# A decoder stack in two interleaved streams: another order of their steps, and fewer matmuls of constants

## What is computed

```
x = layernorm(x + L0_attn(x))                    causal softmax attention, one head
x = layernorm(x + L0_xattn(x, ctx, ctx, mask))   masked attention on ctx, with its own layernorm
x = layernorm(x + L0_ffn(x))                     256 -> 1024 -> 1024 -> 256, weights of +1 and -1
x = layernorm(x + L1_attn(x))                    linear attention, 16 heads, random features (64)
x = layernorm(x + L1_xattn(x, ctx, ctx))         gated scores of 8 heads with running maximum
x = layernorm(x + L1_ffn(x))                     quantized 256 -> 1024, 3-tap convolution, silu, 1024 -> 256
```

## Time and profile before

| | |
|---|---|
| median of 3 runs | 850.7 us (850.16 to 853.18) |
| profiled execution, span of the core | 848.1 us |
| TensorE busy | 787.7 us, 93% |
| TensorE weight loads (beside the matmuls) | 529.7 us |
| VectorE busy | 573.0 us, 68% |
| ScalarE busy | 355.4 us, 42% |
| GpSimd busy | 150.0 us, 18% |
| mean granted TensorE clock | 0.980 of full |

### The profile page before, as it was taken

The page is one execution under the profiler, slowest core; times in us unless marked ns, Lnnn a source line. Parts: engine busy times, 40 slices in busy tenths (PEclk is TensorE's granted clock), DMA queues, the critical chain, the costliest instruction groups (busy, mean ns, idle before and its releaser), DMA issues.

```text
span 848.1 us, 15194 instructions
## 1 busy us (share of the span) xinstructions
PE 787.7 (93%) x6103; PEld 529.7 (62%) x6171; DVE 573.0 (68%) x1470; ACT 355.4 (42%) x641; POOL 150.0 (18%) x231
## 2 busy tenths in 40 slices
PE   9999999999999889999989999999999979988485
PEld 6766556755676756578754666677556756657233
DVE  2458634762476779968889945466356675788786
ACT  3854213342263237573338433244352233483162
POOL 5011102100015210031420020100026120014200
PEclk9999999999999999999999999999999999999698
DMA  9700000010010000111000030000000000000000
GB/s 354 277 2 1 1 1 0 2 26 2 1 51 26 27 2 2 34 67 51 26 1 1 2 98 1 3 1 2 1 1 1 2 2 2 1 1 2 0 25 26
DMA packets 12742, 23.80 MB, mean 28 GB/s; under 512 B 768, under 2 KB 7040, under 8 KB 12416
## 3 DMA queue, kind: packets, MB, share of 16 engines
q1 hardware_dynamic: 12672, 22.82, 7.8%
HBM read 20.72 MB, written 2.10 MB: 27 GB/s over the span
## 4 chain that ended last, share of the span: by engine, by line
PE 75%; DVE 15%; issue 4%; ACT 3%; POOL 2%; DMA 1%; SPq 0%; DVEq 0%; ACTq 0%; POOLq 0%
PE bank L758 13%; PE bank L568 6%; PE bank L576 5%; PE bank L602 5%; PE bank L623 4%; PE bank L856 4%; PE bank L1097 3%; PE bank L1059 3%; PE bank L554 3%; PE bank L768 3%; PE bank L744 2%; PE bank L837 2%; PE bank L803 2%; PE bank L706 2%; PE bank L561 2%
## 5 line engine op out<-in xcount | busy, mean ns | idle before, releaser
L2084 POOL TENSOR_TENSOR rstd<-rstd,minus_half 128x2 f32<-128x2 f32 x56 | 42.7, 763 | 472.5 <-DVE rstd L1195 472.4
L758 PE MATMUL bank<-work,f0w 128*128 128x512 f16 x512 | 115.5, 379 | 0.1
L758 PEld LDWEIGHTS bank<-work,f0w 128*128 128x128 f16 x512 | 49.3, 98 | 58.8 <-issue 1.6
L1405 DVE SCALAR_TENSOR_TENSOR work<-bank,work 128x512 f16<-128x512 f32 x64 | 42.7, 685 | 48.4 <-ACT work L1907 48.3
L1907 ACT ACTIVATE work<-bank 128x512 f16<-128x512 f32 x64 | 37.0, 597 | 67.1 <-PE bank L758 51.0
L554 PE MATMUL bank<-bar_upper,identb 128*128 128x512 bf16 x201 | 57.7, 398 | 6.9 <-ACT work L1932 2.7
L623 PE MATMUL bank<-work 128*128 128x256 f32 x208 | 50.0, 381 | 0.4 <-DVE work L1302 0.4
L1945 ACT ACTIVATE work<-bank 128x512 f32<-128x512 f32 x32 | 19.1, 596 | 60.9 <-PE bank L856 60.9
L1270 DVE TENSOR_REDUCE small<-bank 128x1 f32<-128x512 f32 (+3 forms) x32 | 18.7, 586 | 35.2 <-PE bank L604 32.2
L623 PEld LDWEIGHTS bank<-work 128*128 128x128 f32 x208 | 38.0, 190 | 7.0 <-issue 1.7
L554 PEld LDWEIGHTS bank<-bar_upper,identb 128*128 128x128 bf16 x235 | 22.3, 103 | 32.0 <-issue 9.2
(11 more groups left out here) (303 smaller groups left out, 1776.1 us busy)
## 6 DMA issues: line engine op xcount, KB each, us to landing
work<-in_mask SPq DMA_DIRECT2D x4, 1024.0 KB, 10.3
xT<-in_xT SPq DMA_DIRECT2D x4, 512.0 KB, 4.8
ctxT<-in_ctxT SPq DMA_DIRECT2D x4, 512.0 KB, 4.8
perf_w<-in_k SPq DMA_DIRECT2D x3, 512.0 KB, 10.1
perf_w<-in_perf_w SPq DMA_DIRECT2D x1, 1536.0 KB, 6.4
x<-in_x SPq DMA_DIRECT2D x2, 512.0 KB, 14.1
ctx<-in_w SPq DMA_DIRECT2D x2, 512.0 KB, 12.2
work<-in_w SPq DMA_DIRECT2D x1, 1024.0 KB, 11.9
```

The costliest lines, as they stand in the source:

```text
L758: ins = nc.tensor.matmul(u.bank[:, :], f0w1[:, k, m * P:(m + 1) * P], s.h1[part][:, k, :], start=(k == 0 and part == 0), stop=(k == NF - 1 ...
L1405: low_part(what, m, dst, number + m, lambda o, x, hi: nc.vector.scalar_tensor_tensor(out=o, in0=x, scalar=0.0, in1=hi, op0=ALU.max, op1=AL ...
L2084: nc.gpsimd.tensor_tensor(s.rstd[:, two], s.rstd[:, two], minus_half[:, 0:2], ALU.pow).then_inc(s.rstd_made.sem, 1)
```

## The change

TURNS is another merged order, on all five queues, and KEEP is another table, whose numbers sum to 36 instead of 235. No other line is changed, so all later lines of the changed kernel stand 14 lines higher (L554 becomes L540). A line or two of each table:

```diff
 TURNS = {
     "tensor":
-        "a8 b1 a4 b1 a6 b2 a2 b1 a13 b3 a1 b4 p1 a2 b1 a3 b2 a4 b1 a2 b1 a1 b1 a6 b1 a2 b1 a4 b1 a4 b2 a3 b1 a2 b2 a2 "
+        "a2 b1 a9 b1 a7 b2 a1 b1 a13 b1 a1 b3 p1 b1 a1 b1 a2 b2 a1 b1 a2 b1 a1 b1 a14 b1 a9 b2 a2 b1 a1 b1 a1 b1 a1 b1 "
...
 KEEP = {
-    "quant.hidden6 0 0": 2, "quant.hidden7 0 0": 3, "quant.topT 0 0": 9, "quant.row2 0 0": 8,
...
+    "self.q 0 0": 2, "cross.q1 0 0": 2, "sign.early 0 0": 1, "perf.ft.1 0 0": 1, "quant.turn0 0 1": 2,
+    "quant.topT 0 1": 2, "perf.ft.0 1 0": 1, "perf.score3.0 1 0": 1, "perf.spread.0 1 0": 1, "perf.fk.1 1 0": 1,
+    "perf.ft.1 1 0": 4, "perf.state.1 1 0": 1, "perf.out1 1 0": 1, "mlstm.xT1 1 0": 2, "quant.hidden5 1 0": 1,
+    "perf.spread.0 1 1": 1, "perf.state.1 1 1": 3, "mlstm.out0 1 1": 1, "quant.turn0 1 1": 1, "quant.turn1 1 1": 1,
+    "quant.hidden0 1 1": 1, "quant.taps0 1 0": 1, "quant.topT 1 1": 4
```

More of the change, by code:

```diff
@@ L37 @@
     "tensor":
[8 rows of a table removed]
[L46 removed]
[11 rows of a table removed]
[L58 removed]
[8 rows of a table removed]
[8 rows of a table added]
+    "vector":
[11 rows of a table added]
+    "scalar":
[8 rows of a table added]
     "gpsimd":
[L68 to L69 removed]
+        "a7 b2 a3 b2 a2 b3 a4 b2 a1 b1 a2 b1 a1 b1 a3 b1 a2 b3 a2 b1 a2 b4 a1 b2 a1 b1 a1 b1 a3 b1 a2 b1 a2 b3 a1 b4 a3 "
+        "w1 b2 a2 b1 a1 b2 a6 b13 a2 b2",
     "sync":
[L71 removed]
+        "w1 a1 w3 b1 a1 w2 a1 b1 a1 w1 b1 w1 b1 a5 b2 a2 b5 a2 b2",
 }
 KEEP = {
[19 rows of a table removed]
[5 rows of a table added]
 }
```

3 lines of the change are left out of this document (removed), and 70 rows, old and new, of tables (KEEP, TURNS).

## The result

The changed kernel takes 846.76 us (median of 20 runs, 841.59 to 851.19), the kernel before 851.62 (20 runs, 848.79 to 854.53). The ratio is 0.9949, interval 0.9933 to 0.9964, which is a gain of 4.3 us (3.1 to 5.7). The profiled execution has a span of 844.5 us beside 848.1 before.

A forecast was written before the change was run, and what follows sets the result against it. TensorE, busy 93% of the span, was taken to bound most of the kernel, VectorE 301 to 361 and 427 to 443 us. Eight stretch terms summed to -9.6 us, giving 841.1 us (837 to 845, chance 0.46; wider range 832 to 854).

The forecast's parts named there:

- the price of 0.215 us: Cost of one constant matmul on TensorE at full clock; all 235 cost some 50 us.
- Stretch 1: 0 to 244 us, TensorE full: 12 constants fewer, forecast -2.4 us.
- Rival A: Freed time turns into TensorE waits, also in stretches called full; 846.9 us, chance 0.24.
- stretches 1, 4 and 6: 0 to 244, 361 to 427 and 443 to 679 us, paced by TensorE: forecast -2.4, -1.3 and -2.8 us.
- Stretch 3: 301 to 361 us, VectorE paces: 66 constants fewer, nearly all hidden, L1502 delays VectorE, clock falls; forecast +1.5 us.
- Stretch 7: 679 to 742 us, mixed waits: 10 constants fewer, about half of their 2.1 us in waits; forecast -1.5 us.
- Stretch 8: 742 us to the end: 60 constants fewer, mostly in waits, gains at row2, heads and an eviction; forecast -2.5 us.
- Stretch 5: 427 to 443 us, VectorE paces: 24 constants fewer give 0, longer low clock costs; forecast +0.4 us.
- Stretch 6: 443 to 679 us, TensorE full: 15 constants fewer give 3.2 us, 0.4 taken back for new waits; forecast -2.8 us.
- the 5 us that I had named as a sign: Any stretch changing by more than 5 us would show the method wrong, the order mattering more than the constants.
- Rival B: Slower through TensorE's low clock, at 301 to 361 us (+13 us) and perhaps the end; 852.4 to 858 us, chance 0.18.
- the two conditions that I gave together: Signs of the clock rival: granted clock below 0.8 in both 301 to 361 us and the last 106 us.

The follow-up runs named there:

- constants_at_second_fall: The changed kernel plus 8 constant matmuls ahead of the first stream's quant.topT in the second round (10 in place of 2): 843.8 us, ratio 0.9912.
- kernels with two and with three places: Changed kernel plus 18 constants, at perf.fq.1/fk.1/ft.1 and first stream's topT, second round: 841.2 us; or plus 36, also at the tail: 840.2 us.

## Why the prediction was right or wrong

- **Which stretches TensorE fills, and the price of 0.215 us there:** right. Stretch 1 gave 3.0 us for 12 constants (2.4 forecast), and 18 constants put into full flow cost 3 to 4 us (3.9 by the price). Rival A, in which half of the freed time of full stretches turns into waits, is out, although its 846.9 us is nearly the measured time: it had 3.3 us for stretches 1, 4 and 6, and they gave 9.8.
- **Stretch 3, hidden behind VectorE, with the delay of L1502 and a short fall of the clock:** right for the sum of 301 to 361 us (+1.1, +1.5 forecast), the row of L1488 shows the wait of 1.39 us, and the clock is 0.89. The low level was on from 302 to 309 and from 332 to 339 us, not in the 8 us after 344, 13.7 us in sum, where I had priced one fall of 4 us. That the sum fits is in part luck.
- **"Stretch 7: 10 fewer, 2.1 us, about half in waits, -1.5":** wrong in sign, +1.0. The step that failed is that I asked of a constant only whether it stood on the path, and took one in a wait for free to remove. The row that I had against the clock (7.3 us of idle time in this stretch and still 1.00) was one with the constants in place; without them the waits of 0.7 us became 1.9 and 1.5, and the clock went to 0.53 for 11 us. Putting them back made the stretch 2.5 us shorter in one profile, and together with those of stretch 8 the whole 5 us shorter by the runs (0.9885 beside 0.9949).
- **"Stretch 8: -1.3, -1.1, -0.4, +0.3 for a lower clock near the end":** three gains by order and constants were outweighed by a term that I had at 0.3 us. Measured +2.5, 5.0 us off. The step that failed is the same one: I took the nine constants at row2 as 1.3 us on the path, and the clock of the steps behind them as given. The 1.3 us came (cols start 1.5 us earlier behind the gates), and cols at the lower level took 2.4 us again. Of the 1.1 us at the heads 0.9 appears where the clock is full. I had also read the nine as running at the low clock; the low level ended while they ran, at 755.70 us. For the rest of the stretch I can't say term by term what the clock took: the low intervals lie differently in every execution.
- **"Stretch 5: +0.4":** mis-sized, +2.5. Giving back the old order took 1.5 us off this stretch (+1.0 in place of +2.5), 20 constants in its wait took nothing. The other 1.0 us is there in the old order with the new constants too (+1.0); that it is the clock at L715 fits, and is not shown. I had read the order of VectorE around L1502, and not here, where two steps of the other stream moved ahead of a chain that TensorE waited for anyway.
- **"Stretch 6: -2.8":** mis-sized, -6.3. This is more than the 5 us that I had named as a sign that the order matters more than the constants; here it doesn't. The constants gave what I said: 15 x 0.215 = 3.2. Beside that, before had a fall of the clock here that after does not have, shown below: 4 us at 0.57, that is 1.7 us. Together 4.9, which is just what the old order with the new constants measured in this stretch; the new order gives 1.4 more, where I took 0.4 off for it.
- **The structure of the sum:** the order was to bring about 1 us and the constants the rest. In truth the removal of 200 constants brings nothing in the old order (ratio 1.0011) and the order nothing with the old constants (1.0005). With the new constants the order is worth 0.6% (0.9949 beside 1.0011), because the old constants overran in stretch 3: taking 66 of them out there gave 0.5% by itself.
- **Rival B, the clock:** the mechanism was right and its place wrong. I had put it into 301 to 361 us, where VectorE paces and a low clock costs little, and at the end as an afterthought. It decided from 679 us on. Of the two conditions that I gave together, the clock below 0.8 in the last 106 us was met with 0.76, and the one for 301 to 361 us was not (0.89). The Trainium skill (TensorE: Matmul & The Clock Gate, section "HAM oscillation — how this bites in real kernels") tells of a kernel whose waits are longer than its bursts of matmuls, and in which each next burst starts at the lower clock. The trace of after agrees at 688.70 us, where a wait of 1.91 us is followed by eight matmuls of 2.09 in place of 1.14, and does not at 685.65, where the wait of 1.40 us was followed by full speed.

## What to carry to other kernels

In these runs a matmul of constants cost its full time where TensorE is full (18 of them 3 to 4 us), nothing to speak of where it fits into a wait, and saved time where a wait would otherwise be followed by real TensorE work on the path; so such fillers are placed wait by wait, by the timeline after the reordering, and not carried over from another order. In this kernel taking 200 of them away in the old order changed nothing that could be measured, and 58 put back ahead of nine steps of the new one, where its trace showed the low level, made the gain near three times as large (0.9855 beside 0.9949); 18 of them at two places gave most of that (0.9880). And before counting a faster TensorE as a gain, look up which engine makes its input: at the end of this program a clock of 1.00 in place of 0.50 took 3 us off TensorE's busy time and 1.6 off the way from row2 to down3, because VectorE paces the steps between.

## What the runs showed of the hardware that was not expected

**The clock can fall while TensorE is busy without a gap.** In the kernel before, windows around the fall in the middle of the stretch that TensorE fills:

```profile
625.00:629.00 4.00, 4.00 (x29) 2.87 (x27) 1.20 (x2) 2.21 (x3) 0.00 (x0) 1.00 0.00 0
629.00:633.00 4.00, 3.67 (x23) 2.60 (x24) 0.00 (x0) 1.41 (x3) 2.79 (x5) 0.57 0.00 0
```

TensorE is busy 4.00 of 4 us and the clock falls right behind. From 626.81 to 629.76 us it had run the cols steps (L994 to L1006), matmuls of 8 rows and 8 to 72 columns. The profile calls this busy. Which property of these steps did it was not tried. The fall is there in before and in the two kernels of the last experiments that have the old order in stretch 5, and not in after, nor in either half of the change alone.

**The same instructions fall at other places in another execution.** The kernels after and constants_at_second_fall are the same up to 738 us. In the profile of the first the clock is low from 302 to 309 us, in that of the second it is not, and the second reaches self.q at 361 us 2.6 us earlier. This is more than half of the change's whole effect. The cols of the kernels with two and with three places, above, are a second case: the same instructions up to there, and 5.2 us in one, 2.8 in the other. Single executions of after range over 9.6 us, of before over 5.7: a kernel that leaves more to the clock varies more, and a comparison of stretches by one profile each is good to 2 or 3 us only.
